# Routed experts of an attention and mixture-of-experts layer: hidden chunks split in pairs, down matmuls four chunks behind, eight chunk buffers

## The chip, the cores and the metric

The kernel runs on one core of a Trainium2 chip. The metric is the device time of one launch in microseconds; the runs shown are separate executions of the same program, and their median counts. TensorE is called PE in the profile, VectorE DVE, ScalarE ACT, GpSimd POOL and SyncE SP.

## What is computed

The input is x and a context, both [8, 512, 256] in fp32. The layer is an attention block followed by a feed-forward block with experts, both added to x. Only the routed experts are touched by the change. Cut to what matters:

```
u  = layernorm(x1)                                  # x1: after the attention block
xn = u * rsqrt(mean(u * u) + eps) * g_routed
h  = gelu(xn @ W1_r[e] + b1_r[e])                   # 256 -> 1024, exact gelu, 8 experts
y  = h @ W2_r[e] + b2_r[e]                          # 1024 -> 256
out = x1 + u + shared(u) + sum over the top 2 experts e of gate_e(u) * y_e(u)
```

## The kernel before, in words

The kernel has two stages. The first (to about line 1032) does the attention, the shared experts and the routing, and writes each normalised token to the list of each of its two experts in DRAM (`sorted_tokens`). The second stage, which starts at line 1035, is the routed experts. It works through NT = 39 tiles of T = 256 tokens; each tile belongs to one expert, whose number and place in the list are read from `tile_expert` and `tile_at`. The loop over the tiles is written out in Python, so the program is one straight stream of instructions for each engine, and each engine's order is the order in which its `body(n, i, r)` writes it. Semaphores alone tie the engines together.

Precision is kept by splitting each fp32 operand into a high part, rounded to the matmul's type (`fp32r`), and a low part, the difference. So a product takes three matmuls: high with high, high with low and low with high. Each tile goes through these steps:

- **SP** (`body`, L1091) loads the tokens `xt`, then W1 and W2 of the expert into `raw`, then the bias. There are two buffers of each, so it waits until the weights of the tile two before are split (`t_wlo`, L1096).
- **Weights** are split in M = 8 pieces of 512 columns, 0 to 3 for W1 and 4 to 7 for W2 (NP1 = 4). ACT makes the high part `whi` (L1184) of all but pieces 3 and 7, which POOL makes (L1297); DVE makes the low part `wlo` (L1233).
- **Tokens**: PE transposes them into PSUM at step XSTEP = 3 (`transposes`, L1113), DVE scales them into `xT` (`tokens`, L1242), POOL casts `xhi` (L1304), DVE subtracts `xlo` (`tokens_low`, L1247).
- **Up**: for each of M = 8 hidden chunks of 128, PE runs six matmuls into one of NU = 4 PSUM banks (L1155).
- **Gelu**: ACT writes `hraw` from the bank (L1206), casts `hhi` (L1209), DVE subtracts `hlo` (L1273). There are NHB = 4 chunk buffers.
- **Down** (`second`, L1123): six matmuls for each chunk add into the tile's output bank (L1135). They run LAG = 2 chunks behind the up matmuls, so the down matmuls of the last two chunks of a tile stand among the first up matmuls of the next.
- **Output**: ACT scales the bank by the gate into `yt` (`output`, L1192), and POOL adds the rows to the result in DRAM with two indirect DMAs (`add_up`, L1313).

Step m of a tile, on PE, is up chunk m, then (at m = 3) the transposes, then the down matmuls of chunk m - LAG, or of chunk M - LAG + m of the tile before. ACT and DVE follow the same m: at each step a chunk and one piece of weights. Which piece, and whether it is the next tile's, a small function says:

```
        def piece_of(m):

            return (m - LAG) % M, m >= LAG
```

At LAG = 2 that is pieces 6 and 7 of the same tile at m = 0 and 1, and pieces 0 to 5 of the next tile at m = 2 to 7. The first up matmul of a tile waits for all four W1 pieces of the tile:

```
                    pe.wait_ge(t_xhi, n + 1)
                    pe.wait_ge(t_xlo, n + 1)
                    pe.wait_ge(t_wlo, M * n + NP1)
```

Of the kernel before, what the change touches and what calls it, by code (L numbers as in the profile page):

```python
# [4 lines left out]
fp32 = mybir.dt.float32  # L5
# [14 lines left out]
def xattn_moe_kernel(nc, x, ctxt, ig_w, ig_b, fg_w, fg_b, ln_scale, g_s, W1_s, b1_s, W2_s, b2_s,  # L20
# [39 lines left out]
    with whole:  # L60
# [972 lines left out]


        stage_c = ExitStack()
        NHB = 4
        Cc = lambda name, shape, dt=fp32: sb(stage_c, name, shape, dt)
        PIECE = 2 * WN // M
        NP1 = WN // PIECE
# [45 lines left out]
        with nc.Block() as block:  # L1085
# [26 lines left out]
            def _(pe):  # L1112
# [9 lines left out]

                def second(n, i, m):  # L1123

                    pe.wait_ge(t_hhi, M * n + m + 1)
                    pe.wait_ge(t_hlo, M * n + m + 1)
                    if m % 2 == 0:
                        pe.wait_ge(t_wlo, M * n + NP1 + m // 2 + 1)
                    if m == 0 and n > 1:
                        pe.wait_ge(t_y, n - 1)  # L1130
                    h = m % NHB
                    wsl = slice(WN + m * D, WN + (m + 1) * D)
                    for j in range(TJ):
                        for t, (l, w) in enumerate(((hhi, whi), (hhi, wlo), (hlo, whi))):
                            last = nc.tensor.matmul(  # L1135
                                y_bank[i][j * D // 512][:, (j * D) % 512:(j * D) % 512 + D], l[:, h, j * P:(j + 1) * P],
                                w[i][:, wsl], start=m == 0 and t == 0 and (j * D) % 512 == 0,
                                stop=m == M - 1 and t == 2, skip_group_check=True)
                    last.then_inc(t_step, 1)
# [31 lines left out]
            def _(sc):  # L1171
# [24 lines left out]
                def body(n, i, r):  # L1196
                    if n == 0:
                        for m in range(M - LAG):
                            weights(0, 0, 0, m)
                    sc.wait_ge(t_b1[i], 16 * r + 16)  # L1200
                    for m in range(M):
                        sc.wait_ge(t_up, M * n + m + 1)
                        if not (n == 0 and m < NHB):

                            sc.wait_ge(t_step, M * n + m - NHB + 1)
                        nc.scalar.activation(hraw[:, m % NHB, :], psum[m % NU][:, 0:T], ACT.Gelu,  # L1206
                                             bias=b1[i][:, m:m + 1]).then_inc(t_gelu, 1)
                        sc.wait_ge(t_gelu, M * n + m + 1)
                        nc.scalar.copy(hhi[:, m % NHB, :], hraw[:, m % NHB, :]).then_inc(t_hhi, 1)  # L1209
                        if m == LAG and n > 0:  # L1210
                            output(n - 1, 1 - i, r - 1 + i)
                        piece, ahead = piece_of(m)
                        if not ahead:
                            weights(n, i, r, piece)
                        elif n < NT - 1:
                            weights(n + 1, 1 - i, r + i, piece)
                    if n == NT - 1:
                        output(n, i, r)
# [4 lines left out]
            def _(dve):  # L1223
# [40 lines left out]
                def body(n, i, r):  # L1264
                    if n == 0:
                        tokens(0, 0)
                        tokens_low(0, 0)
                        for m in range(M - LAG):
                            weights(0, 0, m)
                        owners(0, 0)  # L1270
                    for m in range(M):
                        dve.wait_ge(t_hhi, M * n + m + 1)
                        nc.vector.tensor_tensor(hlo[:, m % NHB, :], hraw[:, m % NHB, :],  # L1273
                                                hhi[:, m % NHB, :].bitcast(fp32), ALU.subtract).then_inc(t_hlo, 1)
                        piece, ahead = piece_of(m)
                        if not ahead:
                            weights(n, i, piece)
                        elif n < NT - 1:
                            if m == XSTEP:
                                tokens(n + 1, 1 - i)  # L1280
                            if m == M - 2:
                                tokens_low(n + 1, 1 - i)
                            weights(n + 1, 1 - i, piece)
                            if m == M - 1:
                                owners(n + 1, 1 - i)
                for n in range(NT):
# [3 lines left out]
            def _(pool):  # L1290
# [26 lines left out]
                def body(n, i, r):  # L1317
                    if n == 0:
                        tokens(0, 0)
                        weights(0, 0, 0, BY_POOL[0])  # L1320
                        weights(0, 0, 0, BY_POOL[1])
                    if n < NT - 1:
                        weights(n + 1, 1 - i, r + i, BY_POOL[0])
                    if n > 0:
                        add_up(n - 1, 1 - i)
                    if n < NT - 1:
                        tokens(n + 1, 1 - i)
                        weights(n + 1, 1 - i, r + i, BY_POOL[1])
                    else:
                        add_up(n, i)  # L1330
# [28 lines left out]
```

## Time and profile before

| what | value |
|---|---|
| median of 3 runs | 1432.65 us (1430.29 to 1432.75) |
| the profiled execution, its own time | 1436.01 us |
| its span, first to last instruction | 1434.3 us |
| mean granted TensorE clock over the span | 0.951 |
| PE busy over the span | 1170.9 us (82%) |
| DVE busy | 1026.1 us (72%) |
| ACT busy | 793.5 us (55%) |
| POOL busy | 389.5 us (27%) |

The profile is of one execution. A row of the timeline gives the start in us from the span's start, the length, the engine, the line of the kernel, the operation and its output and inputs; in brackets behind it stands the time in which the engine was idle before it and what ended that. The length of a matmul includes its way through the array, so successive matmuls overlap, and what one costs is the distance to the next start. An instruction of DVE or ACT can also start a little before the record of the one before it ends.

### The profile page before, as it was taken

The page shows a single profiled execution, that of the slowest core. Times are in us where ns is not written, and L with a number is a line of the kernel's source. Part 1 is how long each engine was busy: PE and PEld are TensorE (multiplying, and loading weights), DVE is VectorE, ACT ScalarE, POOL GpSimd, SP SyncE. Part 2 cuts the span into 40 slices and gives each one's busy share as a digit, 9 for nine tenths or more (in the row PEclk, how much of TensorE's full clock was granted, in tenths as well). Part 3 has the DMA queues.
Part 4 walks back from the last instruction along what each step waited for, and adds up shares of the span by engine and source line. Part 5 has one row for each costly group of instructions (what it writes and reads, how often), then busy time and mean ns, then how long its engine had stood idle before and what let it go on. Part 6 is the DMA issues. An engine that isn't in the chain of part 4 may idle for free. (4 is left out here: it accounts for less than half of the span.)

```text
span 1434.3 us, 22326 instructions
## 1 busy us (share of the span) xinstructions
PE 1170.9 (82%) x7861; PEld 1008.2 (70%) x7861; DVE 1026.1 (72%) x2507; ACT 793.5 (55%) x1454; POOL 389.5 (27%) x397
## 2 busy tenths in 40 slices
PE   0363698797897987997978988599999999999996
PEld 0142477576676666775766777589888999899886
DVE  2356659568567676595684654588898889888984
ACT  2101355444553554554544443488888887888785
POOL 2312122041041121221410201144334433443343
PEclk9986799999999999999999998799999999999998
DMA  4899910000010010000000000677777777777772
GB/s 125 220 265 273 288 61 30 30 30 30 30 59 30 20 41 30 30 31 30 30 15 15 31 19 27 213 206 194 194 218 210 198 190 214 216 198 194 205 220 24
DMA packets 172563, 168.08 MB, mean 117 GB/s; under 512 B 48362, under 2 KB 159860, under 8 KB 172452
## 3 DMA queue, kind: packets, MB, share of 16 engines
q1 hardware_dynamic: 120884, 109.43, 25.3%
q10 hardware_dynamic: 37264, 38.54, 10.5%
q0 software_dynamic: 14304, 18.69, 6.3%
q8 instruction: 63, 1.03, 0.3%
q14 instruction: 48, 0.39, 0.1%
HBM read 109.42 MB, written 57.22 MB: 116 GB/s over the span
## 5 line engine op out<-in xcount | busy, mean ns | idle before, releaser
L1233 DVE TENSOR_TENSOR wlo<-raw,whi 128x512 fp32r<-128x512 f32 x312 | 228.2, 732 | 35.1 <-ACT whi L1184 31.4
L1155 PE MATMUL bank<-xhi,whi 128*128 128x256 f32 x624 | 178.8, 287 | 25.5 <-issue 20.2
L1206 ACT ACTIVATE hraw<-bank,b 128x256 f32<-128x256 f32 x312 | 148.2, 475 | 86.2 <-PE bank L1155 53.1
L1273 DVE TENSOR_TENSOR hlo<-hraw,hhi 128x256 fp32r<-128x256 f32 x312 | 183.1, 587 | 17.5 <-ACT hhi L1209 5.7
L973 PE MATMUL bank<-whs,shared_hhi 128*128 128x256 f32 x512 | 150.0, 293 | 50.1 <-DVE shared_hlo L727 50.1
L1135 PE MATMUL bank<-whi,hhi 128*128 128x256 f32 x624 | 180.3, 289 | 12.8 <-issue 11.4
L523 ACT ACTIVATE shared_hraw<-bank,b1s 128x512 f32<-128x512 f32 x128 | 88.1, 688 | 180.8 <-PE bank L988 171.4
L1155 PE MATMUL bank<-xlo,whi 128*128 128x256 f32 x624 | 175.3, 281 | 0.0
L1155 PE MATMUL bank<-xhi,wlo 128*128 128x256 f32 x624 | 175.1, 281 | 0.0
L1135 PE MATMUL bank<-whi,hlo 128*128 128x256 f32 x624 | 173.4, 278 | 0.0
L1135 PE MATMUL bank<-wlo,hhi 128*128 128x256 f32 x624 | 173.3, 278 | 0.0
L727 DVE TENSOR_TENSOR shared_hlo<-shared_hraw,shared_hhi 128x512 fp32r<-128x512 f32 x128 | 89.9, 706 | 114.1 <-ACT shared_hhi L526 107.5
L458 POOL DMA_INDIRECT sorted_tokens<-rowbuf,slots x64 | 66.3, 1036 | 371.9 <-DVEq L808 354.8
L1184 ACT CAST whi<-raw 128x512 fp32r<-128x512 f32 x234 | 143.9, 616 | 17.3 <-DMA raw<-in_L_ffn_W_r_dram 17.3
L1313 POOL DMA_INDIRECT out_dram<-yt,token x78 | 121.3, 1556 | 96.1 <-ACT yt L1192 84.2
L973 PE MATMUL bank<-wls,shared_hhi 128*128 128x256 f32 x512 | 146.8, 287 | 0.0
L973 PE MATMUL bank<-whs,shared_hlo 128*128 128x256 f32 x512 | 146.5, 286 | 0.0
L973 PEld LDWEIGHTS bank<-whs,shared_hhi 128*128 128x128 f32 x512 | 100.0, 195 | 63.5 <-DVE shared_hlo L727 59.3
L1155 PEld LDWEIGHTS bank<-xhi,whi 128*128 128x128 f32 x624 | 118.4, 190 | 32.5 <-issue 32.5
L1297 POOL CAST whi<-raw 128x512 fp32r<-128x512 f32 x78 | 79.2, 1016 | 213.3 <-PE bank L1135 207.1
L1209 ACT CAST hhi<-hraw 128x256 fp32r<-128x256 f32 x312 | 126.8, 406 | 9.9
L988 PE MATMUL bank<-xhs,whs 128*128 128x512 f32 x256 | 117.4, 459 | 17.0 <-DVE xls L746 11.8
(248 smaller groups left out, 2834.7 us busy)
## 6 DMA issues: line engine op xcount, KB each, us to landing
raw<-in_L_ffn_W_r_dram SPq DMA_DIRECT2D x78, 1024.0 KB, 7.8
sorted_tokens<-base ACTq DMA_DIRECT2D x1, 33540.0 KB, 137.6
xt<-sorted_tokens SPq DMA_DIRECT2D x39, 260.0 KB
big<-in_L_ffn_W_s_dram SPq DMA_DIRECT2D x4, 1024.0 KB
xb<-in_x_dram SPq DMA_DIRECT2D x8, 512.0 KB, 4.6
cb<-in_ctx_dram SPq DMA_DIRECT2D x8, 512.0 KB, 3.6
xr<-in_x_dram SPq DMA_DIRECT2D x8, 512.0 KB, 3.6
out_dram<-base ACTq DMA_DIRECT2D x8, 512.0 KB, 2.9
```

What stands on the lines that cost most here:

```text
L523: nc.scalar.activation(hraw[:, k % NHB, :], up_bank[k % 2][:, :], ACT.Gelu, bias=b1s[:, k // M, k % M:k % M + 1]).then_inc(gelu_done, 1)
L727: tt(hlo[:, k % NHB, :], hraw[:, k % NHB, :], hhi[:, k % NHB, :].bitcast(fp32), ALU.subtract).then_inc(hlo_ready, 1)
L973: last = mm(down_bank[j // 2][:, (j % 2) * D:(j % 2 + 1) * D], h[:, k % NHB, j * P:(j + 1) * P], w[:, e, wsl], start=k == 0 and t == 0 and ...
L988: last = mm(up_bank[k % 2][:, :], w[:, e, wsl], x_[:, c, :], start=c == 0 and t == 0, stop=c == KD - 1 and t == 2)
L1135: last = nc.tensor.matmul(y_bank[i][j * D // 512][:, (j * D) % 512:(j * D) % 512 + D], l[:, h, j * P:(j + 1) * P], w[i][:, wsl], start=m = ...
L1155: last = nc.tensor.matmul(ub[:, 0:T], w[i][:, wsl], x_[i][:, k, :], start=k == 0 and t == 0, stop=k == KD - 1 and t == 2)
L1184: nc.scalar.copy(whi[i][:, psl], raw[i][:, psl]).then_inc(t_whi, 1)
L1206: nc.scalar.activation(hraw[:, m % NHB, :], psum[m % NU][:, 0:T], ACT.Gelu, bias=b1[i][:, m:m + 1]).then_inc(t_gelu, 1)
L1209: nc.scalar.copy(hhi[:, m % NHB, :], hraw[:, m % NHB, :]).then_inc(t_hhi, 1)
L1233: nc.vector.tensor_tensor(wlo[i][:, psl], raw[i][:, psl], whi[i][:, psl].bitcast(fp32), ALU.subtract).then_inc(t_wlo, 1)
L1273: nc.vector.tensor_tensor(hlo[:, m % NHB, :], hraw[:, m % NHB, :], hhi[:, m % NHB, :].bitcast(fp32), ALU.subtract).then_inc(t_hlo, 1)
L1313: nc.gpsimd.indirect_dma_start(out=out_r, out_offset=bass.IndirectOffsetOnAxis(ap=token[n % NG][:, j:j + 1], axis=0), in_=yt[i][:, j, :], ...
```

## The change

The routed stage gets NHB = 8 chunk buffers and a LAG of its own, 4 (before, it took the 2 that the shared experts set). At LAG = 4 the same function gives pieces 4 to 7 of the same tile at m = 0 to 3, and pieces 0 to 3 of the next tile at m = 4 to 7. The cast to `hhi` and the subtraction to `hlo` are done once for two chunks, at odd m, on 512 columns. PE waits for them at even chunks only. On DVE, the tokens of the next tile come behind the piece of weights of their step; on POOL, `xhi` comes ahead of piece 3, and piece 7 behind the indirect DMAs.

```diff
--- before.py
+++ after.py
@@ -1033,7 +1033,8 @@
 
 
         stage_c = ExitStack()
-        NHB = 4
+        NHB = 8
+        LAG = 4
         Cc = lambda name, shape, dt=fp32: sb(stage_c, name, shape, dt)
         PIECE = 2 * WN // M
         NP1 = WN // PIECE
@@ -1122,9 +1123,9 @@
 
                 def second(n, i, m):
 
-                    pe.wait_ge(t_hhi, M * n + m + 1)
-                    pe.wait_ge(t_hlo, M * n + m + 1)
                     if m % 2 == 0:
+                        pe.wait_ge(t_hhi, (M * n + m) // 2 + 1)
+                        pe.wait_ge(t_hlo, (M * n + m) // 2 + 1)
                         pe.wait_ge(t_wlo, M * n + NP1 + m // 2 + 1)
                     if m == 0 and n > 1:
                         pe.wait_ge(t_y, n - 1)
@@ -1205,8 +1206,10 @@
                             sc.wait_ge(t_step, M * n + m - NHB + 1)
                         nc.scalar.activation(hraw[:, m % NHB, :], psum[m % NU][:, 0:T], ACT.Gelu,
                                              bias=b1[i][:, m:m + 1]).then_inc(t_gelu, 1)
-                        sc.wait_ge(t_gelu, M * n + m + 1)
-                        nc.scalar.copy(hhi[:, m % NHB, :], hraw[:, m % NHB, :]).then_inc(t_hhi, 1)
+                        if m % 2:
+                            h = m % NHB
+                            sc.wait_ge(t_gelu, M * n + m + 1)
+                            nc.scalar.copy(hhi[:, h - 1:h + 1, :], hraw[:, h - 1:h + 1, :]).then_inc(t_hhi, 1)
                         if m == LAG and n > 0:
                             output(n - 1, 1 - i, r - 1 + i)
                         piece, ahead = piece_of(m)
@@ -1269,18 +1272,21 @@
                             weights(0, 0, m)
                         owners(0, 0)
                     for m in range(M):
-                        dve.wait_ge(t_hhi, M * n + m + 1)
-                        nc.vector.tensor_tensor(hlo[:, m % NHB, :], hraw[:, m % NHB, :],
-                                                hhi[:, m % NHB, :].bitcast(fp32), ALU.subtract).then_inc(t_hlo, 1)
+                        if m % 2:
+                            h = m % NHB
+                            dve.wait_ge(t_hhi, (M * n + m) // 2 + 1)
+                            nc.vector.tensor_tensor(hlo[:, h - 1:h + 1, :], hraw[:, h - 1:h + 1, :],
+                                                    hhi[:, h - 1:h + 1, :].bitcast(fp32), ALU.subtract).then_inc(t_hlo, 1)
                         piece, ahead = piece_of(m)
                         if not ahead:
                             weights(n, i, piece)
                         elif n < NT - 1:
+                            weights(n + 1, 1 - i, piece)
+                        if n < NT - 1:
                             if m == XSTEP:
                                 tokens(n + 1, 1 - i)
                             if m == M - 2:
                                 tokens_low(n + 1, 1 - i)
-                            weights(n + 1, 1 - i, piece)
                             if m == M - 1:
                                 owners(n + 1, 1 - i)
                 for n in range(NT):
@@ -1320,11 +1326,11 @@
                         weights(0, 0, 0, BY_POOL[0])
                         weights(0, 0, 0, BY_POOL[1])
                     if n < NT - 1:
+                        tokens(n + 1, 1 - i)
                         weights(n + 1, 1 - i, r + i, BY_POOL[0])
                     if n > 0:
                         add_up(n - 1, 1 - i)
                     if n < NT - 1:
-                        tokens(n + 1, 1 - i)
                         weights(n + 1, 1 - i, r + i, BY_POOL[1])
                     else:
                         add_up(n, i)
```

DVE, before, from step 3 of a tile to the first instruction behind the last piece of step 7 (here for a tile whose successor uses buffers 0):

```order
L1242 TENSOR_SCALAR xT<-bank7,gr_col 128x256
L1233 TENSOR_TENSOR wlo_0<-raw_0,whi_0 128x512
L1273 TENSOR_TENSOR hlo<-hraw,hhi 128x256
L1233 TENSOR_TENSOR wlo_0<-raw_0,whi_0 128x512
L1273 TENSOR_TENSOR hlo<-hraw,hhi 128x256
L1233 TENSOR_TENSOR wlo_0<-raw_0,whi_0 128x512
L1273 TENSOR_TENSOR hlo<-hraw,hhi 128x256
L1247 TENSOR_TENSOR xlo_0<-xT,xhi_0 128x512
L1233 TENSOR_TENSOR wlo_0<-raw_0,whi_0 128x512
L1273 TENSOR_TENSOR hlo<-hraw,hhi 128x256
L1233 TENSOR_TENSOR wlo_0<-raw_0,whi_0 128x512
L1255 TENSOR_TENSOR gate_2<-xt_0 128x2
```

The five rows of wlo are pieces 1 to 5 of the next tile. The same place with the change:

```order
L1236 TENSOR_TENSOR wlo_1<-raw_1,whi_1 128x512
L1245 TENSOR_SCALAR xT<-bank6,gr_col 128x256
L1245 TENSOR_SCALAR xT<-bank7,gr_col 128x256
L1236 TENSOR_TENSOR wlo_0<-raw_0,whi_0 128x512
L1278 TENSOR_TENSOR hlo<-hraw,hhi 128x512
L1236 TENSOR_TENSOR wlo_0<-raw_0,whi_0 128x512 x2
L1250 TENSOR_TENSOR xlo_0<-xT,xhi_0 128x512
L1278 TENSOR_TENSOR hlo<-hraw,hhi 128x512
L1236 TENSOR_TENSOR wlo_0<-raw_0,whi_0 128x512
L1258 TENSOR_TENSOR gate_2<-xt_0 128x2
```

Here the first wlo is piece 7 of the tile itself, and the four of `wlo_0` are pieces 0 to 3 of the next tile. xlo now stands ahead of the last hlo, and piece 3 is the last split of the tile, behind the hlo of chunks 6 and 7.

POOL, before, two tiles:

```order
L1313 DMA out_0_dram<-yt_0,token_2 4096x256 x2
L1304 CAST xhi_0<-xT 128x512
L1297 CAST whi_0<-raw_0 128x512
L1297 CAST whi_1<-raw_1 128x512
L1313 DMA out_0_dram<-yt_1,token_3 4096x256 x2
```

And with the change:

```order
L1310 CAST xhi_0<-xT 128x512
L1303 CAST whi_0<-raw_0 128x512
L1319 DMA out_0_dram<-yt_0,token_0 4096x256 x2
L1303 CAST whi_0<-raw_0 128x512
L1310 CAST xhi_1<-xT 128x512
L1303 CAST whi_1<-raw_1 128x512
L1319 DMA out_0_dram<-yt_1,token_1 4096x256 x2
L1303 CAST whi_1<-raw_1 128x512
```

Before, a tile's piece 3 (the second whi of the fence) went ahead of the two DMAs, and xhi and piece 7 followed them. Now xhi and piece 3 go ahead, and piece 7 alone follows.

## Rows read from the trace of the kernel before

**Rows 1.** Windows of the routed stage: length; PE, PEld, DVE, ACT, POOL busy; PEclk; DMA
```profile
917.32:930.69 13.37, 13.35 (x100) 13.18 (x101) 12.14 (x27) 11.38 (x25) 3.00 (x4) 0.88 0.99 327
930.69:1409.98 479.29, 446.50 (x3690) 433.79 (x3689) 430.93 (x849) 388.44 (x888) 191.60 (x185) 1.00 0.73 200
1409.98:1423.00 13.02, 12.88 (x108) 12.68 (x108) 6.60 (x17) 8.35 (x20) 3.34 (x2) 1.00 0.19 22
```

**Rows 2.** Chain of waits, up chunk 3 and transposes of a tile (start, us)
```profile
1102.79 0.71 PE bank L1155 x6
1103.49 0.44 PE bank L1119 x4
```

**Rows 3.** Timeline, PE, end of a tile (start us, us; idle before and releaser)
```profile
1108.53 0.35 PE L1135 MATMUL bank<-whi,hhi 128*128 128x256 f32 x1 [0.41 <-issue]
...
1109.29 0.28 PE L1155 MATMUL bank<-xhi,whi 128*128 128x256 f32 x1
...
1111.41 0.36 PE L1155 MATMUL bank<-xhi,whi 128*128 128x256 f32 x1 [0.55 <-issue]
```

**Rows 4.** Timeline, DVE, the same stretch
```profile
1106.88 1.55 DVE L1273 TENSOR_TENSOR hlo<-hraw,hhi 128x256 fp32r<-128x256 f32 x1
...
1109.69 0.68 DVE L1233 TENSOR_TENSOR wlo<-raw,whi 128x512 fp32r<-128x512 f32 x1
1110.30 0.41 DVE L1273 TENSOR_TENSOR hlo<-hraw,hhi 128x256 fp32r<-128x256 f32 x1
1110.63 0.68 DVE L1247 TENSOR_TENSOR xlo<-xT,xhi 128x512 fp32r<-128x512 f32 x1
```

**Rows 5.** Timeline, ACT, around the same tile's end and in the next
```profile
1110.20 0.48 ACT L1206 ACTIVATE hraw<-bank,b 128x256 f32<-128x256 f32 x1 [0.61 <-PE bank L1155]
1110.70 0.41 ACT L1209 CAST hhi<-hraw 128x256 fp32r<-128x256 f32 x1
1111.02 0.61 ACT L1184 CAST whi<-raw 128x512 fp32r<-128x512 f32 x1
...
1116.00 0.84 ACT L1192 ACTIVATE yt<-bank,gate 128x256 f32<-128x256 f32 x2
1116.73 0.62 ACT L1184 CAST whi<-raw 128x512 fp32r<-128x512 f32 x1
1117.24 0.49 ACT L1206 ACTIVATE hraw<-bank,b 128x256 f32<-128x256 f32 x1
```

**Rows 6.** DMA issues of the page (count, KB each, us to landing)
```profile
raw<-in_L_ffn_W_r_dram SPq DMA_DIRECT2D x78, 1024.0 KB, 7.8
```

**Rows 7.** Timeline, DVE and POOL in the first tile
```profile
924.59 0.68 DVE L1233 TENSOR_TENSOR wlo<-raw,whi 128x512 fp32r<-128x512 f32 x1
925.28 0.74 DVE L1273 TENSOR_TENSOR hlo<-hraw,hhi 128x256 fp32r<-128x256 f32 x1
925.95 1.10 DVE L1233 TENSOR_TENSOR wlo<-raw,whi 128x512 fp32r<-128x512 f32 x1
...
924.74 1.01 POOL L1304 CAST xhi<-xT 128x512 fp32r<-128x512 f32 x1 [3.05 <-DVE xT L1242]
925.70 0.81 POOL L1297 CAST whi<-raw 128x512 fp32r<-128x512 f32 x1
```

**Rows 8.** Timeline, POOL, second indirect DMA and the cast behind it
```profile
1105.95 1.55 POOL L1313 DMA_INDIRECT out_dram<-yt,token  x1 [0.30 <-issue]
1106.94 1.19 POOL L1304 CAST xhi<-xT 128x512 fp32r<-128x512 f32 x1
```

**Rows 9.** Timeline, PE, first and fifteenth matmul of the stage
```profile
917.32 0.55 PE L1155 MATMUL bank<-xhi,whi 128*128 128x256 f32 x1 [5.32 <-DVE wlo L1233]
...
920.44 0.28 PE L1155 MATMUL bank<-xhi,wlo 128*128 128x256 f32 x1
```

**Rows 10.** Windows of two stretches of the first stage, PEclk the last column but two
```profile
628.00:636.00 8.00, 5.33 (x33) 4.17 (x32) 7.21 (x33) 3.68 (x6) 0.00 (x0) 1.00 0.00 0
743.00:756.00 13.00, 7.87 (x48) 7.66 (x47) 9.07 (x18) 3.19 (x5) 5.15 (x6) 0.76 0.00 0
```

## The prediction

> **What bounds the kernel now.** The page gives shares over the whole span and does not tell the stages apart, so I read the routed stage by windows first [rows 1], then its chain of waits [rows 2], then one tile of it in order of time on PE, DVE and ACT [rows 3 to 5]. The stage runs from 917.32 to 1423.0. Its 37 middle tiles take 479.29 us, 12.954 us each, with the granted clock at 1.00, PE busy 446.50 of it and DVE 430.93 [rows 1]. A group of six matmuls takes about 0.70 us and the four transposes 0.44 [rows 2], so a tile without a wait is 16 x 0.70 + 0.44 = 11.64 us. The other 1.31 us are two stops: 0.41 before down chunk 4, and 0.55 before the next tile's first up matmul [rows 3], each with some 0.2 us of refill around it. The view calls them "issue" and names nobody; DVE's rows do. hlo of chunk 4 ends at 1106.88 + 1.55 = 1108.43 and PE goes on at 1108.53; xlo ends at 1111.31 and PE goes on at 1111.41 [rows 3, 4]. So PE bounds the stage, and twice a tile DVE is late: xT, xlo and two POOL casts that hold DVE up all fall in the second half of a tile.
>
> **What the change removes.** Per tile 8 hhi casts and 8 hlo subtractions of 256 columns become 4 and 4 of 512. What counts is start to start: on ACT 0.32 after an hhi and 0.52 after a cast of 512 columns, so a pair saves 2 x 0.32 - 0.52 = 0.12 us [rows 5]; on DVE 0.33 against 0.60, so a pair saves 0.06 [rows 4]. Over four pairs ACT gains 0.5 us and DVE 0.25 us a tile. PE's work does not change, so this is worth 0 unless it ends a wait. The two present stops do go: down chunk 4 now has four steps in place of two between it and its up matmuls, and xlo stands ahead of the last pair.
>
> **What it moves, and this decides.** The helper that picks a weight piece uses LAG as well. With 4 in it the W1 pieces 0 to 3 of the next tile are converted at m = 4 to 7, not at 2 to 5, and piece 3 stands in DVE's order behind the hlo of chunks 6 and 7 (the order rows of DVE). PE's first up matmul of a tile waits for all four W1 pieces. So a chain closes through every tile boundary: up chunk 7, Gelu, hhi pair, hlo pair, wlo of piece 3, next tile. PE has one group of six, 0.70 us, to put beside it. Before, W2 pieces stood in that place, which PE wants much later.
>
> **One tile, from its first up matmul (t = 0).** Up chunks start at 0, 1.47, 2.87, 4.27, 6.11, 7.51, 8.91 and 10.31: 1.40 a step, 0.07 of refill in the first, 0.44 for the transposes in step 3. Gelu starts 0.91 after its up chunk (1109.29 to 1110.20) and the cast 0.50 after Gelu [rows 3, 5]. On ACT, Gelu 4 starts at 7.02, two yt follow, whi piece 0 runs from 8.14 to 8.76; Gelu 5 8.66, hhi pair 9.17, whi 1 9.69, Gelu 6 10.21, whi 2 10.60 to 11.22; Gelu 7 11.22, last hhi pair 11.72 to 12.34 (0.62, from whi, which has its shape [rows 5]). On DVE, the hlo of 2 and 3 starts at 6.34, wlo piece 7 6.94, xT 7.54 to 8.41, wlo 0 from 8.79, wlo 2 11.25, xlo 11.85, last hlo pair 12.45, wlo 3 13.05, which ends at 13.73 (0.68 [rows 4]). PE goes on 0.10 later: **13.83 us a tile against 12.954**, with one stop of about 2.1 us at each boundary. The sum:
> - 37 middle tiles x 0.876 = +32.4 us.
> - First tile: 13.37 before [rows 1]. Two down groups leave it (-1.40) and its end gets the 2.1 us; but its own stops, which the busy row does not show, go. That bounds it by 0 and +0.7; I take +0.4 us.
> - Last tile: 13.02 before, with 18 groups; now 20 groups, 14.1, so +1.1 us.
>
> Together +33.9 us. The profiled execution took 1436.01 us, so 1469.9 by it. It lies 3.36 above the median of the runs, so I say 1432.65 + 33.9 = **1466.5 us**.
>
> **What I cost at nothing.** Loads: raw for two tiles on is issued once wlo piece 7 is done, some 8 us into a tile, and piece 0 of it is wanted one tile later; a load lands in 7.8 us [rows 6], which leaves 6 us. If that cover went, ACT's first whi would wait and move the whole chain with it. PSUM: up chunk m waits only for Gelu m - 4, done over 2 us before. The eight buffers come round after eight chunks, of which PE's lag takes four. yt moves from m = 2 to m = 4, and its bank is wanted a tile later. POOL now has xhi and piece 3 ahead of its two indirect DMAs and piece 7 behind them, which is the next point.
>
> **The unknown price: POOL's casts against DVE.** In the first tile, with no indirect DMA ahead, xhi runs from 924.74 to 925.75, and an hlo that started inside it ends at 926.02; whi runs to 926.51, and a wlo inside it ends at 927.05 [rows 7]. DVE stands until the cast is over and then needs 0.27 us (256 columns) or 0.55 (512). A wlo begun 0.15 before the cast was not touched (0.68). In my tile xhi runs from 8.48 to 9.09, so wlo 0 ends at 9.64, whi 3 at 10.13 and the hlo of 4 and 5 at 10.68. wlo 2 waits for ACT until 11.25 anyway: free. The second meeting is whi 7 behind the DMAs: 10.13 + 0.30 + 1.55 + 0.30 + 0.99 = 13.27 [rows 8]. The deciding wlo 3 really begins as the hlo pair ends, at 13.13, and is ahead by 0.14 us. That is thin.
>
> **Rivals.**
> - **B, a POOL cast holds piece 3 up: slower still.** If POOL is 0.14 us earlier (no gap behind its cast, or whi 3 taken before wlo 0), whi 7 starts between 12.5 and 13.1, and behind an indirect DMA such a cast lasted 1.19 [rows 8]. wlo 3 then ends 0.55 after it, the tile takes 14.4 to 14.9, say 14.65: 37 x 1.696 + 1.5 = +64 us, **1497 us**; the top gives 1506. For it: the margin. Against it: whatever in my walk runs late on POOL widens it. The Trainium skill, SBUF — State Buffer, "Who interferes with whom", says that a DVE instruction with two SBUF inputs and a GpSimd instruction that reads SBUF exclude each other, the first to start holding the other for its full length. By that rule the starting order alone chooses between the forecast and B, and the trace agrees (0.27 and 0.55 us after the cast's end [rows 7]).
> - **C, faster.** The boundary is covered: both present stops are gone, nothing takes their place, and a tile takes 11.7: 37 x -1.25 = -46 us, **1386 us**. It holds if wlo 3 ends before t = 11.6, and mine ends at 13.73. Even if the pairs cost what 256 columns do (0.41, then 0.33), the chain gives 10.31 + 0.91 + 0.50 + 0.41 + 0.03 + 0.33 + 0.68 + 0.10 = 13.27, still above 12.954: 37 x 0.32 + 1.1 = +12.8 us, 1445.5. DVE's order speaks against C.
> - **D, no change.** The new stop costs just what the two old ones did. It needs the chain at 12.95, 0.3 under its cheapest.
> - **E, the clock falls in the new stop.** After 5.32 us of standing, PE's first 14 matmuls took 3.12 us, 0.22 each [rows 9], against 0.12: 1.4 us, and 37 times that is +52 us on the forecast, 1518. But a stretch of 8 us with PE busy 5.33 kept a clock of 1.00, and only one with PE busy 7.87 of 13 us shows 0.76 [rows 10]. My tile has 2.1 of 13.83 idle, which is nearer to the first.
>
> **How the numbers follow.** Forecast 0.52, B 0.38, E 0.05, C 0.03, D 0.02. The two likely cases run from 1460 to 1506. For pairs cheaper than I took, bounded by 1445.5, I open the low side to 1456; the high side stands at 1507. The forecast's own range is 1456 to 1476. About 3 us, 0.2%, is what a measurement of this kernel tells from no change. Faster 0.03, same 0.02, slower 0.95.
>
> **What would show it.** In the changed profile: one stop of PE per tile, of some 2 us, ahead of the first up matmul; none ahead of down chunk 4; wlo 3 directly behind an hlo pair of 0.68 us and 0.10 before PE; tiles 13.8 apart. In B that wlo takes 1.1 us or more and tiles are 14.4 apart or more. Tiles under 13.2 apart would prove me wrong: the boundary is then not bound by this chain.

## The result and the profile after

The changed kernel took 1505.07 us in the median (1497.32 to 1516.99, 4 runs), the kernel before 1432.7: the ratio is 1.0514, with a 95% interval of 1.0454 to 1.0575. The profiled execution took 1506.45 us, its span is 1503.7 us. So the kernel is slower by 72 us. The direction is the one forecast, the size is a little over twice the one forecast (+33.9 us).

The page's engine shares, and from the waits in the routed stage that of PE (engine and line, what it waited for; us, times, longest):

```profile
PE 1180.5 (79%) x7861; PEld 1025.1 (68%) x7861; DVE 1011.2 (67%) x2351; ACT 766.9 (51%) x1298; POOL 424.6 (28%) x397
```

```profile
PE bank L1156 <- DVE wlo L1236: 99.1, 39, 5.5
```

PE is 79% busy where it was 82%. The waits view now has a name for the stop: PE waits 39 times for DVE's wlo, once a tile, 99.1 us in all. The stops ahead of down chunk 4 are gone. The windows of the stage (first tile, 37 middle tiles, last tile; then two single tiles; columns as in [rows 1]):

```profile
912.62:926.97 14.35, 11.41 (x76) 11.23 (x77) 10.75 (x20) 9.08 (x18) 3.66 (x4) 0.82 0.82 267
926.97:1476.67 549.70, 459.01 (x3701) 452.62 (x3701) 417.40 (x702) 363.38 (x740) 226.00 (x185) 0.96 0.63 175
1476.67:1492.50 15.83, 15.83 (x120) 15.66 (x120) 5.97 (x12) 8.56 (x17) 3.29 (x3) 0.89 0.19 24
```

```profile
1029.69:1046.07 16.38, 13.39 (x101) 13.22 (x101) 11.38 (x20) 9.89 (x20) 6.03 (x6) 0.90 0.58 157
1076.45:1090.42 13.97, 11.85 (x100) 11.68 (x101) 11.20 (x20) 9.79 (x20) 6.16 (x6) 1.00 0.66 181
```

To compare these with the kernel before, its windows must be cut at the same places. Those of [rows 1] are not: at 930.69 the second up chunk of its second tile starts, and the tile itself starts at 929.21. From tile start to tile start the kernel before has:

```profile
917.32:929.21 11.89, 11.87 (x89) 11.70 (x89) 10.66 (x23) 10.19 (x23) 3.00 (x4) 0.87 0.98 324
929.21:1409.98 480.77, 447.98 (x3700) 435.27 (x3701) 432.41 (x852) 389.63 (x890) 191.60 (x185) 1.00 0.73 200
```

So the 37 middle tiles take 549.70 us where they took 480.77: +68.9 us. The first tile takes 14.35 us for 11.89 and the last 15.8 for 13.0, together +5.3; against that the stage starts 4.7 us earlier, at 912.62, after a first stage that the change does not touch. That makes the 69.4 us between the two spans. But the middle tiles are not alike. Read off PE's first up matmul of each tile, the distances are of four kinds: 13.98 us (15 tiles), 14.84 (9), 15.56 (8) and 16.40 (5). Two single tiles above show it: 13.97 us at a clock of 1.00, and 16.38 at 0.90. Two tile ends, on PE (start, length; idle before and what ended it):

```profile
1209.53 0.36 PE L1156 MATMUL bank<-xhi,whi 128*128 128x256 f32 x1 [2.98 <-DVE wlo L1236]
...
1223.51 0.36 PE L1156 MATMUL bank<-xhi,whi 128*128 128x256 f32 x1 [2.12 <-DVE wlo L1236]
```

On ACT and DVE at the end that came at 1223.51, and on DVE at the one of 1209.53:

```profile
1219.70 0.47 ACT L1207 ACTIVATE hraw<-bank,b 128x256 f32<-128x256 f32 x1
1220.07 0.61 ACT L1185 CAST whi<-raw 128x512 fp32r<-128x512 f32 x1
1220.72 0.48 ACT L1207 ACTIVATE hraw<-bank,b 128x256 f32<-128x256 f32 x1
1221.22 0.62 ACT L1212 CAST hhi<-hraw 128x512 fp32r<-128x512 f32 x1
```

```profile
1206.53 0.68 DVE L1250 TENSOR_TENSOR xlo<-xT,xhi 128x512 fp32r<-128x512 f32 x1
1207.13 0.73 DVE L1278 TENSOR_TENSOR hlo<-hraw,hhi 128x512 fp32r<-128x512 f32 x1
1207.78 1.49 DVE L1236 TENSOR_TENSOR wlo<-raw,whi 128x512 fp32r<-128x512 f32 x1
1209.20 0.55 DVE L1258 TENSOR_TENSOR gate<-xt 128x2 f32<-128x2 f32 x1
...
1221.37 0.68 DVE L1250 TENSOR_TENSOR xlo<-xT,xhi 128x512 fp32r<-128x512 f32 x1
1221.97 0.68 DVE L1278 TENSOR_TENSOR hlo<-hraw,hhi 128x512 fp32r<-128x512 f32 x1
1222.57 0.68 DVE L1236 TENSOR_TENSOR wlo<-raw,whi 128x512 fp32r<-128x512 f32 x1
1223.17 0.96 DVE L1258 TENSOR_TENSOR gate<-xt 128x2 f32<-128x2 f32 x1
```

On POOL at both ends:

```profile
1207.14 1.54 POOL L1319 DMA_INDIRECT out_dram<-yt,token  x1 [0.30 <-issue]
1208.12 1.60 POOL L1303 CAST whi<-raw 128x512 fp32r<-128x512 f32 x1
...
1221.98 2.08 POOL L1319 DMA_INDIRECT out_dram<-yt,token  x1 [0.30 <-issue]
1223.51 1.18 POOL L1303 CAST whi<-raw 128x512 fp32r<-128x512 f32 x1
```

The reader is to see the chain link by link. With the tile's start at 1209.53, Gelu 7 starts at 11.19 us, the hhi pair at 11.69, xlo at 11.84, the hlo pair at 12.44, wlo of piece 3 at 13.04 and ends at 13.72; PE goes on at 13.98. In the tile before, the same wlo takes 1.49 us, not 0.68, and PE stands 2.98 us, not 2.12. In all 14 tiles of that kind the wlo ends 0.59 us behind the end of the second indirect DMA, and 0.45 us before the end of the cast (1208.68, 1209.27 and 1209.72 here).

And where PE has stood, the next matmuls sometimes come at half the pace. At 1033.30 and 1033.51, in a tile that began behind a stop of 2.98 us, they are 0.21 us apart; from 1033.87 they are 0.12 apart. The window below the rows (columns as before) has the granted clock of the slow stretch, 0.50, which is 1.2 of the 2.4 GHz:

```profile
1029.69 0.36 PE L1156 MATMUL bank<-xhi,whi 128*128 128x256 f32 x1 [2.98 <-DVE wlo L1236]
...
1033.30 0.41 PE L1136 MATMUL bank<-wlo,hhi 128*128 128x256 f32 x1
1033.51 0.41 PE L1136 MATMUL bank<-whi,hlo 128*128 128x256 f32 x1
1033.72 0.31 PE L1136 MATMUL bank<-whi,hhi 128*128 128x256 f32 x1
1033.87 0.28 PE L1136 MATMUL bank<-wlo,hhi 128*128 128x256 f32 x1
1033.99 0.28 PE L1136 MATMUL bank<-whi,hlo 128*128 128x256 f32 x1
```

```profile
1030.40:1033.75 3.35, 3.35 (x18) 3.35 (x18) 0.69 (x1) 1.41 (x3) 0.00 (x0) 0.50 0.85 128
```

Split over the 37 tiles, which took 12.994 us each before (480.77 / 37): 37 x (13.98 - 12.994) = 36.5 us for the chain; 14 tiles with the stretched wlo, 14 x 0.86 = 12.0 us; 13 tiles that ran partly at 1.2 GHz, 13 x 1.57 = 20.4 us. Together 68.9 us, the difference of the windows. From here on, "lock" stands for a DVE subtraction that is held up beside POOL's work, as in the 14 tiles.

### The profile page after: what moved, and what is told of

It reads as the page before. It is cut to its first block and busy times, and to the rows that moved or that the text cites. A ratio compares the mean times of both kernels' runs of the same rounds, so it can differ in the third digit from the quotient of the medians.

```text
span 1503.7 us, 21854 instructions
## 1 busy us (share of the span) xinstructions
PE 1180.5 (79%) x7861; PEld 1025.1 (68%) x7861; DVE 1011.2 (67%) x2351; ACT 766.9 (51%) x1298; POOL 424.6 (28%) x397
## 3 DMA queue, kind: packets, MB, share of 16 engines
q8 instruction: 62, 1.02, 0.3%
## 5 line engine op out<-in xcount | busy, mean ns | idle before, releaser
L1156 PE MATMUL bank<-xhi,whi 128*128 128x256 f32 x624 | 184.2, 295 | 99.1 <-DVE wlo L1236 99.1
L1156 PEld LDWEIGHTS bank<-xhi,whi 128*128 128x128 f32 x624 | 124.2, 199 | 106.1 <-issue 106.1
L1156 PE MATMUL bank<-xlo,whi 128*128 128x256 f32 x624 | 180.5, 289 | 0.0
L1156 PE MATMUL bank<-xhi,wlo 128*128 128x256 f32 x624 | 180.4, 289 | 0.0
L1136 PE MATMUL bank<-whi,hlo 128*128 128x256 f32 x624 | 178.9, 287 | 0.0
L1136 PE MATMUL bank<-wlo,hhi 128*128 128x256 f32 x624 | 178.5, 286 | 0.0
L1278 DVE TENSOR_TENSOR hlo<-hraw,hhi 128x512 fp32r<-128x512 f32 x156 | 117.4, 753 | 79.9 <-ACT hhi L1212 76.7
L1319 POOL DMA_INDIRECT out_dram<-yt,token x78 | 143.0, 1833 | 31.2 <-issue 17.8
L1310 POOL CAST xhi<-xT 128x512 fp32r<-128x512 f32 x39 | 24.3, 624 | 359.4 <-DVE xT L1245 359.4
L1156 PEld LDWEIGHTS bank<-xlo,whi 128*128 128x128 f32 x624 | 123.6, 198 | 0.0
```

What stands on the lines that cost most here:

```text
L1136: last = nc.tensor.matmul(y_bank[i][j * D // 512][:, (j * D) % 512:(j * D) % 512 + D], l[:, h, j * P:(j + 1) * P], w[i][:, wsl], start=m = ...
L1156: last = nc.tensor.matmul(ub[:, 0:T], w[i][:, wsl], x_[i][:, k, :], start=k == 0 and t == 0, stop=k == KD - 1 and t == 2)
L1278: nc.vector.tensor_tensor(hlo[:, h - 1:h + 1, :], hraw[:, h - 1:h + 1, :], hhi[:, h - 1:h + 1, :].bitcast(fp32), ALU.subtract).then_inc(t_ ...
L1319: nc.gpsimd.indirect_dma_start(out=out_r, out_offset=bass.IndirectOffsetOnAxis(ap=token[n % NG][:, j:j + 1], axis=0), in_=yt[i][:, j, :], ...
```

## The experiments

Every kernel computes the whole layer. Times are medians, ratios are to the kernel before with their 95% intervals; "tile" is the mean distance of the first up matmuls of neighbouring tiles in the profile of each (over 38 distances, the first tile among them), 12.96 us in the kernel before and 14.84 in the changed one.

| run | weights' lag, down lag, chunks | us | ratio (interval) | tile, us |
|---|---|---|---|---|
| changed kernel | 4, 4, pairs | 1505.07 | 1.0514 (1.0454 to 1.0575) | 14.84 |
| e1: piece 3 ahead of the last pair | 4, 4, pairs | 1447.08 | 1.0114 (1.0085 to 1.0142) | 13.42 |
| e2: single chunks | 4, 4, single | 1581.05 | 1.1040 (1.1009 to 1.1071) | 16.83 |
| e3: piece 7 ahead of the indirect DMAs | 4, 4, pairs | 1516.30 | 1.0586 (1.0565 to 1.0607) | 15.10 |
| e5: piece 7 cast by ACT | 4, 4, pairs | 1483.36 | 1.0353 (1.0329 to 1.0376) | 14.32 |
| e6: LAG = 2 | 2, 2, pairs | 1506.89 | 1.0515 (1.0493 to 1.0537) | 14.78 |
| e7: the orders alone, on the kernel before | 2, 2, single | 1439.51 | 1.0045 (1.0025 to 1.0064) | 13.14 |
| e10: weights' lag 3, single chunks | 3, 4, single | 1438.81 | 1.0031 (1.0017 to 1.0044) | 13.08 |
| e4: weights' lag 3 | 3, 4, pairs | 1422.49 | 0.9935 (0.9913 to 0.9958) | 12.73 |
| e8: e4, pair 4 and 5 behind xlo | 3, 4, pairs | 1407.81 | 0.9829 (0.9803 to 0.9855) | 12.31 |
| e9: e8, xlo at step 4 | 3, 4, pairs | 1407.33 | 0.9814 (0.9793 to 0.9835) | 12.28 |
| e11: e8, piece 7 cast by ACT | 3, 4, pairs | 1408.64 | 0.9831 (0.9804 to 0.9857) | 12.31 |

### Is it the place of piece 3? (e1, e4)

e1 moves one instruction of DVE, in step 7:

```diff
                     for m in range(M):
+                        if m == M - 1 and n < NT - 1:
+                            weights(n + 1, 1 - i, BY_POOL[0])
                         if m % 2:
...
-                        elif n < NT - 1:
+                        elif n < NT - 1 and m < M - 1:
                             weights(n + 1, 1 - i, piece)
```

> Changed kernel, with one move: at step 7 DVE splits weight piece 3 ahead of the hlo of chunks 6 and 7 (same instructions, same work). Theory (the boundary chain runs through Gelu 7, hhi pair, hlo pair, piece 3): piece 3 no longer waits for the pair and stands directly behind xlo, so it ends at about 13.1 of a tile and not at 13.7, PE's stop falls by 0.6 us, 37 x -0.6 = -22 us, and if the shorter stop keeps the clock up, as much again: 1463 to 1483 us. Rival (the stop is something else, such as the wait for xhi or xlo or for ACT): 1505 us as before.

Measured: 1447.08 us, better than the range given. Two tile starts on PE in its profile:

```profile
1044.34 0.36 PE L1156 MATMUL bank<-xhi,whi 128*128 128x256 f32 x1 [1.51 <-DVE wlo L1236]
...
1057.71 0.36 PE L1156 MATMUL bank<-xhi,whi 128*128 128x256 f32 x1 [1.51 <-DVE wlo L1236]
```

The tiles are 13.37 us apart, 0.61 below 13.98, just what one instruction of 0.60 start to start would give. PE's stop is 1.51 us here (1.51 to 1.63 over the tiles), and none of the 37 tiles shows the slow matmuls, and none a stretched piece 3. The lock itself is still there: in 16 of the 37 tiles the hlo pair, which now stands behind piece 3, takes 1.48 us, but PE's first up matmul does not wait for it. So the one move takes off the 0.6 us, and with it both extras: 58 us in all, of which 22 are the chain. That the chain runs through the pair and piece 3 is shown; that a shorter stop also keeps the clock up is seen here for the first time.

e4 takes the same thought further and gives the weights a lag of their own:

```diff
         LAG = 4
+        WLAG = 3
...
-            return (m - LAG) % M, m >= LAG
+            return (m - WLAG) % M, m >= WLAG
...
-                        for m in range(M - LAG):
+                        for m in range(M - WLAG):
```

(the last on ACT and on DVE)

> Changed kernel, but the weight pieces follow a lag of their own, 3 in place of 4: pieces 0 to 3 of the next tile at steps 3 to 6, piece 4 at step 7. Down matmuls stay four chunks behind, pairs and eight buffers stay. Theory (the loss is where LAG put piece 3, nothing else): piece 3 and xlo are done at about 11.5 of a tile, PE hardly stops, tiles of 11.8 to 12.3 against 12.954 in the kernel before, 1390 to 1410 us, below both kernels. Rival (ACT's first piece now waits for the last down matmuls of the tile before, or DVE is late all the same): 1430 us or more.

Measured: 1422.49 us, below the kernel before, though not as far as expected. The waits of PE in its stage:

```profile
PE bank L1157 <- DVE xlo L1251: 33.2, 38, 1.6
```

PE stands 38 times, 0.87 us each, now for xlo. By DVE's rows it comes late because of the two casts of POOL (a wlo and an hlo pair beside them take 1.04 and 1.02 us for 0.69) and because the hlo pair of chunks 4 and 5 stands ahead of it; e8 below tests the second alone. Of the rival, the half that holds is that DVE is late all the same; its other half, ACT waiting for the last down matmuls, is not what PE stands for. Both kernels say the same: the change's loss lies in where LAG put the weights, not in the down matmuls being four chunks behind.

### What do the pairs do? (e2, e10, e6)

e2 undoes the pairs and nothing else:

```diff
-                        if m % 2:
-                            h = m % NHB
-                            sc.wait_ge(t_gelu, M * n + m + 1)
-                            nc.scalar.copy(hhi[:, h - 1:h + 1, :], hraw[:, h - 1:h + 1, :]).then_inc(t_hhi, 1)
+                        sc.wait_ge(t_gelu, M * n + m + 1)
+                        nc.scalar.copy(hhi[:, m % NHB, :], hraw[:, m % NHB, :]).then_inc(t_hhi, 1)
```

and the same on DVE and in PE's waits.

> Changed kernel with the casts and subtractions done chunk by chunk again, on 256 columns; LAG 4, eight buffers and the orders stay. Theory: the chain at the boundary gets shorter by the difference between 512 and 256 columns (0.62 to 0.41 on ACT, 0.60 to 0.33 on DVE), about 0.45 us a tile, less what DVE's four extra instructions add: tiles of 13.4 to 13.7 without lock and clock, 1470 to 1495 us. Rival (the pairs save work that counts, and LAG is the cost alone): the same or slower than 1505 us.

Measured: 1581.05 us, 76 us above the changed kernel: my theory missed by far and in sign. One tile end of its profile (the tile from 1062.58 to 1077.99, one of two without slow matmuls; granted clock 0.99), on PE, ACT, DVE and POOL:

```profile
1062.58 0.36 PE L1156 MATMUL bank<-xhi,whi 128*128 128x256 f32 x1 [3.58 <-DVE wlo L1234]
...
1077.99 0.55 PE L1156 MATMUL bank<-xhi,whi 128*128 128x256 f32 x1 [3.56 <-DVE wlo L1234]
```

```profile
1074.31 0.47 ACT L1207 ACTIVATE hraw<-bank,b 128x256 f32<-128x256 f32 x1
1074.80 0.41 ACT L1210 CAST hhi<-hraw 128x256 fp32r<-128x256 f32 x1
```

```profile
1075.04 1.35 DVE L1248 TENSOR_TENSOR xlo<-xT,xhi 128x512 fp32r<-128x512 f32 x1
1076.32 0.82 DVE L1274 TENSOR_TENSOR hlo<-hraw,hhi 128x256 fp32r<-128x256 f32 x1
1077.06 0.68 DVE L1234 TENSOR_TENSOR wlo<-raw,whi 128x512 fp32r<-128x512 f32 x1
```

```profile
1074.26 1.54 POOL L1315 DMA_INDIRECT out_dram<-yt,token  x1 [0.30 <-issue]
1075.24 1.60 POOL L1299 CAST whi<-raw 128x512 fp32r<-128x512 f32 x1
```

The tile takes 15.41 us, 1.43 more than 13.98. Gelu 7 starts at 11.73 of the tile and not at 11.19: a cast starts 0.49 behind the Gelu that it waits for (1074.31 to 1074.80), where in the changed kernel whi comes 0.37 behind Gelu 6 (1219.70 to 1220.07), and the casts of single chunks cost ACT more than the pairs. Together that is 0.54; DVE, which waits for ACT's piece 2, reaches xlo 0.62 later (12.46 of the tile for 11.84). The other part is on DVE: POOL's last cast now meets xlo (1.35 for 0.68) and the last hlo (0.82 for 0.42), both ahead of piece 3, in every tile. That is 1.07 us more, less 0.27 for the shorter hlo: 0.62 + 0.80 = 1.42 of the 1.43. So the chain's links of 256 columns were shorter, as I had it, and the engines reached it later by more. And with a stop of 3.57 us, 35 of the 37 middle tiles run partly slow and take 16.9 us or more.

e10 asks the same with piece 3 out of the way: e2's edit made in e4. Against e2 it is (with `WLAG` used in the same places as in e4):

```diff
         LAG = 4
+        WLAG = 3
```

> Weight lag 3 and down matmuls four chunks behind (the version at 1422 us), with casts and subtractions chunk by chunk on 256 columns. With weight lag 4, single chunks cost 1.4 us a tile more than pairs, without the clock. Theory (pairs free ACT and DVE, which are late at the boundary): slower than with pairs by 0.5 to 1.4 us a tile, 1440 to 1475 us. Rival (the pairs hardly matter once piece 3 is out of the way): 1415 to 1430 us.

Measured: 1438.81 us, 13.08 us a tile for 12.73. The pairs are worth 0.35 us a tile here, 16 us; my range began at 1440. So the pairs are a gain, in both settings, but no fixed one. I had counted the casts and subtractions alone, not that four times a tile ACT no longer waits for the end of a Gelu (0.37 to its next instruction in place of 0.50). That this makes up the 0.35 us is argued from the rows; no run takes it apart.

e6 sets both lags back in the changed kernel.

```diff
-        LAG = 4
+        LAG = 2
```

> Changed kernel with LAG = 2 again, for the down matmuls and the weight pieces; pairs, eight buffers and the orders on DVE and POOL stay. Theory (the pairs need the lag): the down matmuls of an even chunk want a pair whose second Gelu is only 0.7 us of PE work back, so PE stops some 0.7 us ahead of every even chunk, four times a tile, but not 2.1 us at the boundary: tiles of 14 to 15 us, 1475 to 1510 us. Rival (the pairs are a gain that LAG = 4 hides): below 1432 us.

Measured: 1506.89 us. The stops of PE:

```profile
PE bank L1136 <- issue: 84.4, 153, 0.9
```

153 stops for 39 tiles, four a tile, ahead of the even down chunks, 0.55 us each. The theory holds and the size too. With a lag of 2 the pairs are a loss, and none of the middle tiles shows the slow matmuls although PE loses as much: its stops are short and many.

### The orders alone (e7)

```diff
                         elif n < NT - 1:
+                            weights(n + 1, 1 - i, piece)
+                        if n < NT - 1:
                             if m == XSTEP:
                                 tokens(n + 1, 1 - i)
                             if m == M - 2:
                                 tokens_low(n + 1, 1 - i)
-                            weights(n + 1, 1 - i, piece)
```

and on POOL as in the change.

> The kernel before with only the change's two moves of order: on DVE the tokens behind the weight piece of their step, on POOL xhi ahead of piece 3 and piece 7 behind the indirect DMAs. Theory: POOL's casts then meet DVE a little earlier and xlo stands one piece later, so PE's stop ahead of the next tile grows by the 0.6 us of one piece and the one ahead of chunk 4 shrinks: -10 to +15 us, 1422 to 1448 us. Rival (the orders are what makes the changed kernel slow): 1480 us or more.

Measured: 1439.51 us, inside the range: 0.18 us a tile. As expected, PE's stop ahead of the next tile grows (1.16 us for 0.55) and the one ahead of chunk 4 is gone. The orders cost little.

### Who stretches the last subtraction? (e3, e5)

e3 lets POOL cast piece 7 ahead of the indirect DMAs, behind piece 3.

```diff
                         weights(n + 1, 1 - i, r + i, BY_POOL[0])
+                        weights(n + 1, 1 - i, r + i, BY_POOL[1])
                     if n > 0:
                         add_up(n - 1, 1 - i)
-                    if n < NT - 1:
-                        weights(n + 1, 1 - i, r + i, BY_POOL[1])
-                    else:
+                    if n == NT - 1:
```

> Changed kernel with POOL's cast of weight piece 7 ahead of the two indirect DMAs. 14 of 37 tiles had the deciding subtraction of piece 3 stretched from 0.68 to 1.49 us. Theory 1 (my case B: the cast of piece 7 holds it): the cast is then done by 11 us of a tile, no piece 3 is stretched, -12 us: about 1493 us. Theory 2 (the second indirect DMA itself holds it: the stretched ones end 0.59 us behind its end): the DMAs run some 0.6 us later and still lie beside piece 3; stretches stay, in more or fewer tiles, 1490 to 1530 us.

Measured: 1516.30 us. No piece 3 is stretched, so theory 1 had that right, but the kernel did not win the 12 us. Two tile starts, and of DVE ahead of the second a pair, the wlo of pieces 1 and 2, and that of piece 3:

```profile
1076.40 0.36 PE L1156 MATMUL bank<-xhi,whi 128*128 128x256 f32 x1 [2.56 <-DVE wlo L1236]
...
1090.81 0.35 PE L1156 MATMUL bank<-xhi,whi 128*128 128x256 f32 x1 [2.54 <-DVE wlo L1236]
```

```profile
1086.20 0.93 DVE L1278 TENSOR_TENSOR hlo<-hraw,hhi 128x512 fp32r<-128x512 f32 x1
1087.05 1.70 DVE L1236 TENSOR_TENSOR wlo<-raw,whi 128x512 fp32r<-128x512 f32 x2
...
1089.88 0.68 DVE L1236 TENSOR_TENSOR wlo<-raw,whi 128x512 fp32r<-128x512 f32 x1
```

Its tiles are 14.41 us apart without a slow clock: the cast now holds up the two wlo of pieces 1 and 2 (1.70 us, where the changed kernel has 1.28), and that reaches the boundary. PE's stop is 2.5 to 2.6 us in every tile, and 16 of the 37 middle tiles run partly slow. Since the DMAs had also moved against DVE, e3 does not tell the cast from the DMA. e5 does: it leaves every other instruction of POOL at its time and gives the cast to ACT.

```diff
-        BY_POOL = (3, 7)
+        BY_POOL = (3,)
```

(and POOL's calls for piece 7 go)

> Changed kernel with weight piece 7 cast by ACT, in step 3 where ACT has room, and not by POOL; POOL keeps xhi, piece 3 and the two indirect DMAs, at the same times. Theory 1 (the cast behind the DMAs holds piece 3's subtraction, case B of the prediction): none of the last subtractions is stretched to 1.49 us, tiles of 14.84 and 16.40 us are gone, 1490 us. Theory 2 (the second indirect DMA holds it): about as many tiles (14 of 37) are stretched as before, 1500 to 1510 us. Under both, tiles without it stay at 13.98.

Measured: 1483.36 us, 22 below the changed kernel and a little below the 1490 of theory 1. A tile end in its profile, DVE, POOL and PE:

```profile
1226.05 0.68 DVE L1278 TENSOR_TENSOR hlo<-hraw,hhi 128x512 fp32r<-128x512 f32 x1
1226.65 0.68 DVE L1236 TENSOR_TENSOR wlo<-raw,whi 128x512 fp32r<-128x512 f32 x1
1227.25 0.15 DVE L1258 TENSOR_TENSOR gate<-xt 128x2 f32<-128x2 f32 x1
```

```profile
1226.06 2.08 POOL L1319 DMA_INDIRECT out_dram<-yt,token  x1 [0.30 <-issue]
```

```profile
1227.59 0.36 PE L1156 MATMUL bank<-xhi,whi 128*128 128x256 f32 x1 [2.12 <-DVE wlo L1236]
```

The second indirect DMA stands 1.53 us ahead of the tile's end as in the changed kernel (1221.98 against 1223.51), and no subtraction in 37 tiles is stretched. Some of its tiles have the DMA at 1.54 us and the hlo pair at 0.73, which in the changed kernel always came with the stretched wlo; here such a tile takes 14.04 us, not 14.84. Even the small owner instruction is back at 0.15 from 0.96. So it takes the cast that queues behind the DMA to hold DVE up; the DMA alone does not. Tiles without it stay at 13.98, and eight of the 37 still run partly slow.

### A version that beats both (e8, e9, e11)

e8 is e4 with the hlo pair of chunks 4 and 5 given out behind xlo in step 6, since PE wants it only after the next tile's first up chunk:

```diff
-                        if m % 2:
+                        if m % 2 and (m != M - 3 or n == NT - 1):
                             low_pair(n, m)
...
                                 tokens_low(n + 1, 1 - i)
+                                low_pair(n, M - 3)
```

(`low_pair` holds the wait and the subtraction as they were)

> The version with weight lag 3, with the hlo pair of chunks 4 and 5 moved behind xlo on DVE. In it PE still stopped 0.85 us a tile for xlo (tiles of 12.71). Theory: xlo comes 0.6 to 1.0 us earlier, the stop is gone, and the pair is still in time for down chunk 4, 0.7 us after the tile's start: tiles of 11.8 to 12.2, 37 x -0.7 = -26 us on 1422, so 1390 to 1405 us. Rival (DVE as a whole is the bound of that version, and the pair now stops PE instead): 1415 us or more.

Measured: 1407.81 us, 1.7% below the kernel before, and somewhat above the range of the theory. PE's waits in it:

```profile
PE bank L1157 <- DVE xlo L1251: 18.2, 38, 1.5
```

The stop for xlo fell from 0.87 to 0.48 us a tile. The rest is behind ACT: DVE waits 0.53 us for whi of piece 1. Two tries to take that as well gave nothing. e9, on e8:

```diff
-                            if m == M - 2:
+                            if m == M - 4:
                                 tokens_low(n + 1, 1 - i)
+                            if m == M - 2:
                                 low_pair(n, M - 3)
```

> The fastest version so far (weight lag 3, hlo pair of chunks 4 and 5 behind piece 3 and xlo; 1408 us, tiles of 12.3, a stop of 0.45 us for xlo), with xlo moved from step 6 to step 4 on DVE. Theory: DVE there waits 0.53 us for ACT's piece 1, and xlo fills that hole, so piece 3 ends 0 to 0.4 us sooner: tiles of 11.9 to 12.3, 1393 to 1408 us. Rival: POOL's cast of piece 3 holds xlo up at that place and nothing is won, or it gets slower: 1408 to 1420 us.

Measured: 1407.33 us, no different from e8. xlo fills the hole, and PE waits for wlo instead, 0.41 us a tile (15.2 us in 37 waits). Neither way of putting it moved the end. e11 is e8 with e5's edit, piece 7 cast by ACT:

> The version at 1408 us with piece 7 cast by ACT, so that no cast of POOL stands behind the indirect DMAs. Theory: at this lag that cast holds up only the small owner instructions (0.95 in place of 0.15 us), which PE does not wait for, and ACT gets 0.5 us more to do in step 2: no change, 1403 to 1413 us. Rival (DVE's backlog reaches the boundary and the lock is part of it): 1385 to 1400 us.

Measured: 1408.64 us. The lock is off the path here: the theory.

## Why the prediction was right in direction and wrong in size

- **The bound, and what the pairs remove.** PE with two late answers of DVE per tile: this stood, and both stops went as said. That the pairs save 0.5 and 0.25 us a tile and are worth 0 was too small a view. e2 and e10 put them at 1.4 and 0.35 us a tile (0.80 of the 1.4 is the lock that e2 runs into). Against the kernel before that is no gain in the changed kernel, but without it the changed kernel would be the 1581 us of e2.
- **What it moves.** The step that decided was right: piece 3 behind the last pair, one group of PE beside the chain. e1 shows it by moving that one instruction.
- **The walk through a tile.** Gelu 7 at 11.22, xlo at 11.85, hlo pair at 12.45, wlo at 13.05, end at 13.73 were forecast; 11.19, 11.84, 12.44, 13.04 and 13.72 were measured. The last link missed: I took 0.10 us from DVE's end to PE, from xlo, and it was 0.26. So 13.83 became 13.98. The base was misread too: 12.954 comes from the window that starts one up chunk into the second tile, and a tile took 12.994. The term of +32.4 us measures 36.5.
- **First and last tile.** +0.4 and +1.1 were forecast. Measured +2.5 and +2.8. The first tile took 11.89 us before and not 13.37, by the same misreading; the last tile's 15.8 holds one stretch of slow clock, and 15.8 - 1.6 = 14.2 is the 14.1 of the sum.
- **POOL's cast (B), the step that failed first.** I made an all-or-nothing choice of the starting order, with the chance 0.38, and took "not touched". It was neither: 14 of 37 tiles, 12.0 us, where the forecast's sum has nothing for it. B's price per tile stood (14.4 to 14.9 given, 14.84 measured), but by luck, for its mechanism did not. B wanted the cast to start before the wlo; by the record the wlo starts 0.34 us ahead of the cast (1207.78, 1208.12) and is held all the same. B let the wlo go 0.55 us behind the cast's end; it ends 0.45 us before it, and 0.59 behind the DMA's. What parts the two kinds of tile lies further up: in all 37 the DMA's recorded start lies within 0.1 us behind that of the last hlo pair, and either the pair takes 0.73 and the DMA 1.54 (stretched), or 0.68 and 2.08 (not), the cast coming 0.98 or 1.53 us behind the DMA's start. In e2 the DMA starts 0.17 us ahead of the subtraction next to it, takes 1.54 in nearly every tile, and the instruction behind is held in all 37. So the two start level, and which kind a tile is was not to be had from a walk to 0.1 us. The Trainium skill, SBUF — State Buffer, "Who interferes with whom", has the first to start hold the other for its whole length. That two-input subtractions and a POOL cast exclude each other agrees (e5, with no cast, has no stretch); the rule by starting order does not fit the recorded starts of this pair, at least not where the cast is queued behind an indirect DMA. The profile calls its spans on POOL rough, so the recorded start may not be the one that counts. How the port is handed over there stays open.
- **The clock (E), the step that failed worst.** I gave it 0.05, by nearness to a stretch with two stops of together 2.67 us in 8, and priced it for all tiles or none. It came in 13 of 37, at 1.57 us each (I had 1.4): 20.4 us, again with nothing for it in the forecast's sum. What PE did before it fell is in the tiles: of the 14 that began behind a stop of about 2.98 us, 9 ran partly slow; of the 23 behind one of 2.12 us, 4. Of 36 tiles each in the other runs (the second tile, which begins behind a longer stop, left out): in e1 (1.51 to 1.63 us) none, in e5 (2.1 to 2.3) 7, in e3 (2.5 to 2.6) 15, in e2 (3.57) 34. My comparison was with two stops of 1.16 and 1.51 us. So B and E were not rivals to the forecast but came on top of it, each in a part of the tiles, and by these counts B's longer stops raised E.
- **Why the range still held it.** By luck: its top, 1507, was B in all tiles. The measured 1505 is another mixture: in the middle tiles 36.5 us of chain, 12.0 of lock, 20.4 of clock.
- **C and D**, faster and no change, had nothing for them. The cheapest chain of 13.27, which opened the low side, left out that the engines reach its links later with single chunks: e2 has them, and its tile took 15.41 without the clock.

## What to carry to other kernels

A constant that sets one distance in a software pipeline often sets others: look for every use, and ask for each moved item who waits for it and what now stands in front. Here one lag served the down matmuls and the weight pieces, and a lag of 3 for the second turned +5.1% into -0.7%, and -1.7% with one more reorder. When a loop's boundary is bound by a chain, its length buys more than its time: at 2 to 3 us of standing, PE began to lose clock in some rounds, so here the last 0.6 us of the stop, together with what hung on them, cost 58 us where their length alone is 22.

## What was not expected of the hardware

- A cast of POOL that is queued behind an indirect DMA holds a DVE subtraction for 0.81 us (0.68 to 1.49), in 14 of 37 like tiles and not in the others, and lets it go 0.45 us before its own end. The DMA itself grows from 1.54 to 2.08 us in the tiles where DVE is not held.
- Stops of one length do not all cost clock. Behind 2.12 us it fell in 4 of 23 tiles, behind 2.98 in 9 of 14, behind 1.5 in none. The changed kernel's runs also scatter more, though with four runs each that is only a hint: 1497.32 to 1516.99 us, against 1446.83 to 1453.12 for e1 and 1407.14 to 1411.82 for e8.
- PE came back 0.26 us behind the end of the wlo that it waited for, in tiles of both kinds, and 0.10 us behind xlo in the kernel before. It goes with which of the two comes last, and not with the kernel: 0.10 behind xlo in e4, e7, e8, e10 and e11 too, 0.26 behind wlo in nearly all tiles of e1, e2, e3, e5 and e9, and e9 differs from e8 only in the place of xlo. Why it does is open.
